# A two-layer graph network on one core: the opening of its first layer cut into quarters, with bias products and transposes moved behind the adjacency's

## The reference, cut to what matters

```python
# x: 2048 x 256, adj: 2048 x 2048 integers
h = maximum(layernorm(x), 0)
mask = adj > 0
agg = mask @ h / maximum(mask.sum(1), 1)
x = x + relu(concat(h @ W_self + b_self, agg @ W_nb + b_nb) @ W_comb + b_comb)
h = maximum(layernorm(x), 0)
state = h
for _ in range(5):                        # gated graph step, A = adj
    a_in  = A   @ (state @ in_W.T  + in_b)
    a_out = A.T @ (state @ out_W.T + out_b)
    r, z = sigmoid([a_in, a_out, state] @ r_W.T + r_b), sigmoid([...] @ z_W.T + z_b)
    h_hat = tanh([a_in, a_out, r * state] @ h_W.T + h_b)
    state = (1 - z) * state + z * h_hat
out = x + tanh(state @ o1_W.T + o1_b) @ o2_W.T + o2_b
```

## Time and profile before

| | |
|---|---|
| median of 3 runs | 1275.48 us (1275.31 to 1275.56) |
| the profiled execution's own time | 1275.44 us |
| its span in the profile | 1273.6 us, so 1.84 us lie around it |
| PE busy | 1244.5 us (98%) |
| DVE, ACT, POOL busy | 724.5, 278.8, 3.0 us |
| mean granted clock of PE | 0.993 |
| first `mean_sum` begins | 40.30 us |
| last `mean_sum` of the first block begins | 58.97 us |

### The profile page before, as it was taken

How to read it: one execution, slowest core, us unless ns; L and a number is a source line. 1 busy time by engine, 2 the same in 40 slices (tenths; PEclk the granted TensorE clock), 3 DMA queues, 4 the chain that set the end, 5 groups by cost and what they waited for, 6 DMA issues and landing times.

```text
span 1273.6 us, 12854 instructions
## 1 busy us (share of the span) xinstructions
PE 1244.5 (98%) x4922; PEld 603.5 (47%) x4922; DVE 724.5 (57%) x1222; ACT 278.8 (22%) x544; POOL 3.0 (0%) x9
## 2 busy tenths in 40 slices
PE   7999999999998999999999999999999999999998
PEld 5666654444443444444444444444444444444445
DVE  5577654065647458258547538745744863672674
ACT  4756211010013012022302103211211330120121
POOL 0000000000000000000000000000000000000000
PEclk9899999999998999999999999999999999999999
DMA  8454093015292820840380281075066019106201
GB/s 302 138 172 156 34 346 140 1 41 223 115 347 108 330 99 1 289 173 0 145 318 0 101 301 61 1 279 184 0 217 245 1 56 350 56 33 232 87 1 66
DMA packets 44410, 182.97 MB, mean 144 GB/s; under 512 B 3521, under 2 KB 13506, under 8 KB 28610
## 3 DMA queue, kind: packets, MB, share of 16 engines
q1 hardware_dynamic: 43344, 178.40, 38.4%
q0 software_dynamic: 720, 3.67, 0.8%
q10 hardware_dynamic: 290, 0.14, 0.1%
HBM read 147.07 MB, written 35.13 MB: 143 GB/s over the span
## 4 chain that ended last, share of the span: by engine, by line
PE 83%; DVE 6%; issue 1%; ACT 0%; DVEq 0%
PE bank L308 81%; DVE GZ L1308 1%; PE bank L471 1%; DVE GZ L1311 1%; DVE u_buf L1334 1%; DVE RT L1246 0%; DVE RT L1248 0%; DVE GZ L1321 0%; DVE GR L1244 0%; DVE RT L1249 0%; DVE ST L1284 0%; DVE GH L1281 0%; PE bank L424 0%; DVE work L1190 0%; DVE ST L1192 0%
## 5 line engine op out<-in xcount | busy, mean ns | idle before, releaser
L308 PE MATMUL bank<-slot,LF 128*128 128x512 f16 x1792 | 391.0, 380 | 0.0
L308 PEld LDWEIGHTS bank<-slot,LF 128*128 128x128 f16 x1792 | 175.8, 98 | 211.4 <-issue 4.5
L308 PE MATMUL bank<-X,W 128*128 128x512 f32 x384 | 180.5, 592 | 0.0
L308 PE MATMUL bank<-XT,W 128*128 128x512 f32 x288 | 136.2, 595 | 5.2 <-DVE u_buf L1334 5.2
L308 PEld LDWEIGHTS bank<-X,W 128*128 128x128 f32 x384 | 72.5, 190 | 88.0 <-issue 86.9
L308 PE MATMUL bank<-work,WG 128*128 128x512 f32 x224 | 97.1, 592 | 0.0
L308 PE MATMUL bank<-AT,SN 128*128 (+1 forms) x256 | 97.0, 379 | 0.0
L308 PE MATMUL bank<-A,SN 128*128 (+1 forms) x256 | 97.0, 379 | 0.0
L308 PEld LDWEIGHTS bank<-XT,W 128*128 128x128 f32 x288 | 53.8, 190 | 75.5 <-issue 62.9
L1211 DVE TENSOR_TENSOR u_buf<-bank,m_buf 128x512 f32<-128x512 f32 x16 | 11.1, 691 | 130.7 <-PE bank L308 130.7
L726 ACT ACTIVATE m_buf<-bank 128x512 f32<-128x512 f32 x40 | 23.8, 596 | 235.4 <-PE bank L308 235.4
(11 more groups left out here) (170 smaller groups left out, 1368.3 us busy)
## 6 DMA issues: line engine op xcount, KB each, us to landing
slot<-quad_d SPq DMA_DIRECT2D x112, 1024.0 KB, 5.5
WG<-in_adj SPq DMA_DIRECT2D x32, 512.0 KB, 4.3
quad_d<-AT SPq DMA_DIRECT2D x14, 1024.0 KB, 5.0
quad_d<-A SPq DMA_DIRECT2D x14, 1024.0 KB, 6.3
SN<-in_x SPq DMA_DIRECT2D x2, 1024.0 KB, 10.5
x_d<-SN POOLq DMA_DIRECT2D x4, 512.0 KB, 2.9
x1o<-x_d SPq DMA_DIRECT2D x1, 2048.0 KB, 8.3
out<-res SPq DMA_DIRECT2D x4, 512.0 KB, 3.0
```

Source lines behind the costliest of these rows:

```text
L308: return pe.matmul(o, l, r, start=start, stop=stop, skip_group_check=again)
```

## The change

1. DVE clears a small buffer `idle16`, and PE multiplies it with itself 10 times (`WARM`) into a bank that nobody reads, ahead of its first real product.
2. ACT takes one square root of a constant before its first copy.
3. `newton`'s result is multiplied by `SCALE`, so `h32` is written already scaled by 2048 and without the maximum. The maximum is taken by whoever reads it: ACT's Relu for the first high half, GpSimd for the high halves of the three other quarters, DVE in `low`, and ACT and DVE when they move `turn_h` (with a factor 1/`SCALE`).
4. DVE writes only quarters 0 and 1 and the low half of quarter 0 ahead of its loop; `low(1)` and `normal(2)` come in step 2, `low(2)` and `normal(3)` in step 5, `low(3)` in step 8 (`HIGH_AT`). `mean_sum` waits for one quarter at a time.
5. `turn_h(0..3)` moves behind `mean_sum` of steps 5, 7, 9, 11 (`TURN_AT`), in banks 6 and 7 only, and its movers four steps later in ACT's and DVE's loops.
6. The products for `bias0` and the gate bias columns move behind `mean_sum(1)` (`BIAS_AT`). GpSimd scales and adds the gate weights beforehand (`scaled`), so 12 one-column products stand in place of 24. GpSimd's queue has this work ahead of the store of `fusedS`, and the three high halves behind it.

```diff
+            for w in range(2):                       # GpSimd
+                pool.wait_ge(ld_w[w], 32)
+                for j in range(2):
+                    nc.gpsimd.tensor_scalar(scaled[:, w, j, :], wgR[w][:, j, :], col[:, 2 * w + j:2 * w + j + 1], None,
+                                            ALU.mult).then_inc(gsum, 1)
+                pool.wait_ge(gsum, 3 * w + 2)
+                nc.gpsimd.tensor_tensor(scaled[:, w, 0, :], scaled[:, w, 0, :], scaled[:, w, 1, :],
+                                        ALU.add).then_inc(gsum, 1)
             pool.wait_ge(fused_out, 8)
             pool.dma_start(fused_d, fusedS).then_inc(st_fused, 16)
+            pool.wait_ge(h_hi, 1)
+            for q in range(1, 4):
+                pool.wait_ge(h_ready, q + 1)
+                nc.gpsimd.tensor_scalar(hi_lo[:, BT * q:BT * q + BT, 0, :], h32[:, BT * q:BT * q + BT, :], 0.0, None,
+                                        ALU.max).then_inc(h_hi, 1)
...
+            pe.wait_ge(warm, 2)                      # PE
+            for e in range(WARM):
+                mm(bank[7][:, :], idle16[:, 0:P], idle16[:, :], True, True)
...
+            def biases():
+                pe.wait_ge(left_ready, 1)
+                pe.wait_ge(fused_out, 8)
+                for j in range(4):
+                    mm(bank[7][:, 0:D], L0[:, j, :], wcR[:, j, :], j == 0, False)
+                mm(bank[7][:, 0:D], cst[0:1, C_ONE:C_ONE + P], b_combR[0:1, :], False, True)
+                pe.wait_ge(gsum, 6)
+                for w in range(2):
+                    for t in range(6):
+                        last = mm(bank[6][:, 6 * w + t:6 * w + t + 1], scaled[:, w, 0, t * P:t * P + P],
+                                  cst[:, C_ONE:C_ONE + 1], True, True)
+                last.then_inc(setup_done, 1)
...
                 if i == 0:
                     pe.wait_ge(id16_ready, 1)
-                    pe.wait_ge(hT_act, NB)
-                    pe.wait_ge(hT_dve, NB)
+                    pe.wait_ge(fused_out, 8)
...
+                if m % BT == 0 and b == 0:
+                    pe.wait_ge(h_hi, m // BT + 1)
+                    pe.wait_ge(h_lo, m // BT + 1)
                 if m == 0 and b == 0:
-                    pe.wait_ge(h_hi, 4)
-                    pe.wait_ge(h_lo, 4)
                     pe.wait_ge(w12_out, 1)
...
             for i in range(NT * NB):
                 mean_sum(i)
+                if i == BIAS_AT:
+                    biases()
+                if i in TURN_AT:
+                    turn_h(TURN_AT.index(i))
...
+            act.wait_ge(warm, 2)                     # ACT
+            nc.scalar.activation(nrm[:, 2, 0:1], nrm[:, 3, 0:1], ACT.Sqrt)
...
+            act.wait_ge(h_ready, 1)
+            nc.scalar.activation(hi_lo[:, 0:BT, 0, :], h32[:, 0:BT, :], ACT.Relu).then_inc(h_hi, 1)
+            act.wait_ge(w12_sum, 1)
             for w in range(2):
+                ins = copy(W12[:, 2 * w:2 * w + 2, :].rearrange("p k n -> p (k n)"), bank[w][:, :])
+            ins.then_inc(w12_out, 1)
...
+            rs = newton(NT, 1)                       # DVE
+            link(v.tensor_scalar(rs, rs, SCALE, None, ALU.mult))
+
+            def normal(q):
                 for t in range(BT * q, BT * q + BT):
                     ins = v.tensor_scalar(h32[:, t, :], xs[:, t, :], mv[:, t, 0:1], nrm[:, 3, t:t + 1],
                                           ALU.subtract, ALU.mult)
+                ins.then_inc(h_ready, 1)
...
+                       scalar=0.0, in1=hi_lo[:, BT * q:BT * q + BT, 0, :],
+                       op0=ALU.max, op1=ALU.subtract).then_inc(h_lo, 1)
...
+            normal(0)
+            normal(1)
+            low(0)
...
             for i in range(NT * NB + 1):
+                if i in HIGH_AT:
+                    low(HIGH_AT.index(i) + 1)
+                if i in HIGH_AT[:2]:
+                    normal(HIGH_AT.index(i) + 2)
+                if i - 4 in TURN_AT:
+                    turned_h(TURN_AT.index(i - 4))
                 if i:
                     make_mask(i - 1)
```

More of the change, by code:

```diff
@@ L39 @@
 H2_AT = 12
+HIGH_AT = [2, 5, 8]
+TURN_AT = [5, 7, 9, 11]
+BIAS_AT = 1
+WARM = 10
 def graph_net(nc, x, adj, w_in, w_out, wg_t, w0_t, w_comb, w_o, cols, b_comb, o2_b, consts, out):
@@ L119, in graph_net @@
         diag = work[:, 8192:16384].bitcast(FP16).rearrange("p (w t n) -> p w t n", w=2, t=NT)
+        idle16 = work[:, 0:2 * BN].bitcast(FP16)
         xs = SN[:, :, :, :].rearrange("p t s d -> p t (s d)").bitcast(FP32)
@@ L141, in graph_net @@
         h32 = AT[:, 1, :, :].rearrange("p t n -> p (t n)").bitcast(FP32).rearrange("p (t d) -> p t d", t=NT)
+        scaled = AT[:, 2, :, :].rearrange("p t n -> p (t n)").bitcast(FP32)[:, 0:4 * GATES].rearrange(
+            "p (w j n) -> p w j n", w=2, j=2)
         fusedS = AT[:, 3, :, :].rearrange("p t n -> p (t n)").bitcast(FP32)[:, 0:4 * GATES].rearrange(
@@ L160, in graph_net @@
         setup_done = sem("setup_done")
+        w12_sum, gsum, gcol_out = sem("w12_sum"), sem("gsum"), sem("gcol_out")
+        warm = sem("warm")
         var_ready, sqrt_ready = sem("var_ready"), sem("sqrt_ready")
@@ L324, in turn_h @@
                 pe.wait_ge(h_ready, b + 1)
-                if b < 2:
-                    pe.wait_ge(fused_out, 2 * b + 6)
-                else:
-                    pe.wait_ge(hT_act, b - 1)
-                    pe.wait_ge(hT_dve, b - 1)
+                if b == 0:
+                    pe.wait_ge(gcol_out, 1)
+                else:
+                    pe.wait_ge(hT_act, b)
+                    pe.wait_ge(hT_dve, b)
                 for f in range(FT):
                     for q in range(BT):
-                        last = pe.transpose(bank[4 + 2 * (b % 2) + f][:, q * P:q * P + P],
+                        last = pe.transpose(bank[6 + f][:, q * P:q * P + P],
                                             h32[:, BT * b + q, f * P:f * P + P], ident)
@@ L343, in _ @@
                                   wcR[:, 2 * w + j, :], j == 0, j == 1)
[L345 to L357, removed]
-            turn_h(2)
-            turn_h(3)
+            last.then_inc(w12_sum, 1)
+            def biases():
[10 more added lines that the diff above has]
+                last.then_inc(setup_done, 1)
             def turn_adj(i):
@@ L404, in dense @@
                 pe.wait_ge(agg_dve, b + 1)
+                if b == 0:
+                    pe.wait_ge(hT_act, NB)
+                    pe.wait_ge(hT_dve, NB)
                 if b > 0:
@@ L808, in _ @@
                 k = 2 * (i // 4 + 1) + i % 4 // 2
+                if i == 0:
+                    move_adj(0)
                 if k < 8 * NB:
@@ L812, in _ @@
                     block_end(i // NT - 1)[0]()
-                if i % 2 == 0:
+                if i % 2 == 0 and i:
                     move_adj(i)
+                if i - 4 == BIAS_AT:
+                    combined()
+                if i - 4 in TURN_AT:
+                    move_h(TURN_AT.index(i - 4))
                 if i >= NT and i % NT in STAGE_AT:
@@ L955, in variance @@
                 v.tensor_scalar(nrm[:, 0, 0:n], mv[:, 0:n, 1], EPS, None, ALU.add).then_inc(var_ready, 1)
+            v.memset(idle16, 0.0).then_inc(warm, 1)
+            v.memset(nrm[:, 3, 0:1], 1.0).then_inc(warm, 1)
             row_stats(range(NT), 0)
@@ L974, in newton @@
                 link(v.reciprocal(rs, sc))
-            newton(NT, 1)
-            for q in range(4):
+                return rs
+            rs = newton(NT, 1)
+            link(v.tensor_scalar(rs, rs, SCALE, None, ALU.mult))
+            def normal(q):
                 for t in range(BT * q, BT * q + BT):
```

34 lines of the change are left out of this document (13 added, 21 removed).

## The result

The changed kernel takes 1277.82 us in the median of 11 runs (1276.65 to 1279.47), against 1275.48 for the kernel before (1274.49 to 1276.48, 11 runs): ratio 1.002, interval 1.001 to 1.0029. It is slower by 2.3 us, where 1272.7 was forecast and 1277.0 was the top of the range. The profiled execution took 1277.3 us, with a span of 1275.5.

What follows compares the result with a forecast made beforehand. DVE's chain was taken to bound the opening and PE's own work the loop. A lead of 4.25 us less 1.5 for the clock gave -2.75 against 1275.44, so 1272.7 us; the range for 8 in 10 was 1270.6 to 1277.0.

Steps and rivals of the forecast that it cites:

- Step 1: Opening, to the first mean_sum: it starts at 26.45 us in place of 40.30; idle products cost nothing either way.
- Step 2: Second mean_sum: starts at 30.15 us against 42.35, waiting for mask 1 behind low(1) and normal(2) on DVE.
- Step 3: PE work moved into the loop: 7.95 us, so the first block's last mean_sum starts at 54.7 us, 4.25 earlier.
- Step 4: Clock low when the second mean_sum starts: costs 1.5 us, between bounds of 0.85 and 2.3.
- The sum: Whole run: -4.25 + 1.5 = -2.75 us against 1275.44, giving 1272.7 us.
- The forecast's own range: Whole run: 1271.9 to 1273.4 us, from the two bounds of the clock's cost.
- The rivals: Four other outcomes: clock never low 0.15, DVE and GpSimd collide 0.30, clock stays low 0.10, GpSimd too slow 0.08.
- GpSimd's case: High half of T us delays mask 1; from T = 2.6 each further us costs one; 1274 to 1284; chance 0.08.
- the low clock's: Clock stays low through the bias products and third mean_sum: 6.45 us lost, 1277.6 us; chance 0.10.
- The collision: DVE and GpSimd hold each other up, mask 0 at 27.05 us: run 1273.65 to 1274.9; chance 0.30.
- What would show it: Profile signs: second mean_sum near 30.2 waiting on DVE's mask, block's last near 56; clock 0.5 past 36 means low clock.

Runs made afterwards that it cites:

- e4: Changed kernel without the 10 idle products at the start and PE's wait for them: 1277.77 us, ratio 1.0018.
- e10: e3 with the high halves of quarters 1 to 3 on ScalarE in place of GpSimd: 1268.85 us, ratio 0.9947.
- e3: Changed kernel with the bias products ahead of the first mean_sum in place of behind the second: 1269.85 us, ratio 0.9955.
- e12: e11 and e10 together: 1267.43 us, ratio 0.9938.
- e11: e3 with one idle product of 384 columns behind each gate bias column: 1269.78 us, ratio 0.9958.
- e2: Changed kernel with 14 idle products ahead of the first mean_sum and 15 ahead of the second, in PE's gaps: 1274.06 us, ratio 0.9986.
- e9: e2 with one idle product of 384 columns behind each of the 12 gate bias columns: 1273.75 us, ratio 0.9986.
- e7: e3 with DVE's added work later, HIGH_AT = [4, 6, 9]: 1272.11 us, ratio 0.9976.
- e8: e7 with the gate bias columns ahead of the bias row: 1274.84 us, ratio 0.9993.

## Why the prediction was wrong

- **Step 1** held. `newton` began at 20.71 (20.40 forecast; the loads of `x` landed 0.3 us later), the first mask at 26.17 (26.1), the first `mean_sum` at 27.03 (26.45), the 0.5 being mask 0's longer time beside GpSimd. The idle products are worth nothing (e4), as said.
- **Step 2 failed in one term**: GpSimd's pass over 1024 elements, taken as 1.22 us from a DVE row and bounded at 2.44. It took 3.57, over the bound and over the 2.6 from which, as the rival said, each further us counts. It also began 0.4 later than forecast, and `low(1)` began 0.5 behind its end, at 29.07 in place of 27.2. DVE waited 1.49, and the second `mean_sum` came 1.7 late. Twice the slowest DVE row was no bound at all: a different engine's duration can't be bounded by a multiple chosen by hand. At the milestone e10 against e3 and e12 against e11 both price GpSimd's three passes at 1.8 us (in the medians 1.0 and 2.4).
- **Step 3** held in its order, but was sized too small by 0.9 us: at clock 1.00 the bias row takes 2.53 in place of 2.1, the columns 2.70 in place of 2.3, four `turn_h` 3.6 in place of 3.5. The bias row was priced at the pace of a long stream, though its last two instructions take 0.63 from start to start in the kernel before too (24.53 to 25.16). The columns were priced by a count of 20 in a stretch of 2 us, which may well take in those that reach over its ends; at e2's 0.1125 each, 18 fit. No wait of PE stood inside steps 2 to 15, as forecast.
- **Step 4 failed most**: it allowed one low spell at 1.5 us, and the clock cost 4.1 in two. The first (to 36.9 us) cost 2.4 by e2, over both rows that should bound it: 5 us of work without a gap, from 31.85 on, still ran low, where the clock had come back after 1.7 us in one row and some 4.6 in the other. The second, behind the columns, cost 1.6 by e9 and was not in the sum at all, without a reason given. The earlier trace rows had shown the fall in the midst of 48 such instructions, and I used it only for the rival. That e2 wins 2.4 us from the second to the last `mean_sum` with products that nobody reads shows the first term by itself; e9 shows the second.
- **The sum.** 1.7 (step 2), 0.9 (step 3) and 4.1 - 1.5 = 2.6 (step 4) are 5.2 us, and the milestone is 2.38 + 2.75 = 5.1 off the forecast. The forecast's own range is 0.1 off as well: 0.85 and 2.3 for the clock give 1272.0 and 1273.5.
- **The rivals.** None of the four alone: the outcome is GpSimd's case at T = 3.57 and two thirds of the low clock's together (4.1 of 6.45 us, but in two spells, and the first ended in the bias row). Each had been given a chance as if the others didn't happen, so their sum, -4.25 + 1.7 + 0.9 + 4.1 = +2.4 us, stood outside the range. The collision did not come as forecast: mask 0 started at 26.17, in the midst of GpSimd's pass. But it took 0.5 us longer, and the pass beside `low(0)` took 0.6 to 0.8 longer than the other two, so a part of step 2's 1.7 may be the collision's; no run takes the two apart.
- **What would show it** named the right places: the second `mean_sum` waited for mask 1, clock 0.5 past 36 us was the sign of the low clock, and the gain at 59 us was not there.

The Trainium skill ("SBUF — State Buffer", section "Who interferes with whom") calls the ports that DVE and GpSimd share an exclusive lock, held by whoever issues first for the whole instruction. Here a mask beside a GpSimd pass took 0.80 or 1.10 us in place of 0.29, the longer one up to the end of the pass, and GpSimd took 3.57 with `low(0)` at its start and 2.76 with DVE quiet, which agrees that they hold each other up; but mask 0, issued 1.2 us into the pass, ended 1.6 us before the pass did, so the hold was not for the whole instruction.

The Trainium skill ("GPSIMD Engine Reference", section 4.1) calls a one-input pass roughly line rate. The trace disagrees: 2.76 us at best for 1024 elements, four times DVE's 0.69 and more per element than the two-input adds of 768 in 1.81. The measurement decides.

Left open: why the high half takes as long as it does (its output is half precision in pieces of 256 with gaps; nothing was tried with another form), how much of it is the collision, what exactly lets the clock fall behind the columns, and behind a wait of 3.1 us in e7 but not in e8, and what sets the length of the spell near 391 us.

## What to carry to other kernels

Before work is moved into a stretch that TensorE bounds, fill TensorE's gaps with it: the same bias products, moved from behind the second `mean_sum` to ahead of the first, made the run 8.0 us shorter. In the changed kernel a gap on TensorE was paid twice, once for itself and once in half pace behind it (2.4 us; after e8's wait of 3.1 us there was no such cost), and a run of 24 one-column instructions was paid in the same way (1.6 us); price a spell of low clock at the worst row or above, and ask whether there are two. And an engine whose arithmetic the trace doesn't show has no price from its neighbours: measure one instruction first, and look whether a rival's condition (here 2.6 us) lies inside what it could be. And when two remedies seem to help or hide each other by 1 us in medians, look in the traces where that 1 us lies before a cause is named.

## What was not expected

- Holding the clock in e3 (e11) gave 0.1 us, since PE, now ahead, waited 1.91 us for mask 4.
- Of the 1.4 us between e10 and e12, the traces have 0.2 in the opening that was edited and 1.3 some 300 us behind the milestone, in a low spell of another length.
- A `tensor_scalar` with a scalar per partition on GpSimd took 2.2 us for 768 elements, longer than the two-input add of as many (1.81).
- Idle products are worth nothing at the start of the run (e4) and 3.8 us in the median in the two gaps (e2).
